# Turning the values product round, with GpSimd normalising, in a two-layer windowed-attention kernel

## What is computed

```
h = shift_token(x)                     # the second half of the columns comes from the row before
q, k, v = split(h @ wqkv)              # 8 heads of 64
q, k = rotary(l2norm(q) * qs, l2norm(k) * ksc)
# windows of 128 rows; each looks at itself and at the window before: 256 keys
attn = softmax(mask(8 * q @ k.T))
o = attn @ v
x = x + o @ wo
h = layernorm(shift_token(x)) @ w1 + b1   # 256 -> 2 x 682
a, g = split(h)
x = x + (a * gelu(g)) @ w2 + b2
```

## Time and profile before

| | |
|---|---|
| median of 3 runs | 3229.55 us (3192.76 to 3246.99) |
| profiled execution: span, which is its own time | 3224.0 us |
| TensorE busy | 96% |
| VectorE busy | 76% |
| ScalarE busy | 58% |
| GpSimd busy | 37% |
| mean granted TensorE clock | 0.969 |
| a steady pair of steps (odd and even) | 42.83 us |

### The profile page before, as it was taken

One profiled execution on the slowest core, in us unless ns is written; L12 is line 12 of the kernel. 1 busy time (PEld: TensorE's weight loads), 2 busy tenths in 40 slices (PEclk: granted clock), 3 DMA queues, 4 the chain that ended last, 5 costly groups with the idle time before them and its releaser, 6 DMA issues.

```text
span 3224.0 us, 71318 instructions
## 1 busy us (share of the span) xinstructions
PE 3082.3 (96%) x23040; PEld 2745.2 (85%) x23040; DVE 2444.6 (76%) x7393; ACT 1877.0 (58%) x4750; POOL 1190.4 (37%) x1303
## 2 busy tenths in 40 slices
PE   8999799999999999999999999999999999999997
PEld 6777588988888898989888888988898888889896
DVE  3566687777777777878777788878787878788885
ACT  3455365665565665656655666656566656566663
POOL 3455343333333333323233334334343344343342
PEclk7799899999999999999999999999999999999998
DMA  4344400000000000000002211001010011010000
GB/s 139 111 138 156 157 25 20 23 24 21 23 24 21 22 20 23 24 21 23 22 23 77 80 42 31 28 26 31 24 30 28 27 31 31 24 31 27 27 28 17
DMA packets 139639, 137.09 MB, mean 43 GB/s; under 512 B 15256, under 2 KB 124912, under 8 KB 137968
## 3 DMA queue, kind: packets, MB, share of 16 engines
q1 hardware_dynamic: 139248, 132.18, 13.0%
HBM read 80.22 MB, written 51.92 MB: 41 GB/s over the span
## 4 chain that ended last, share of the span: by engine, by line
PE 66%; DVE 13%; issue 6%; ACT 2%; DVEq 1%; DMA 1%; POOL 1%; SPq 0%; ACTq 0%; POOLq 0%
PE p_values L1320 11%; PE p_wide L95 10%; PE p_wide L97 9%; PE p_wide L96 9%; PE p_turn L1303 5%; PE p_mixed L95 4%; PE p_mixed L96 3%; PE p_mixed L97 3%; PE p_turn L1277 3%; PE p_score L95 2%; DVE prob L1112 2%; DVE rope_sin L1130 2%; DVE rope_cos L1126 2%; PE p_values L1346 1%; PE p_score L96 1%
## 5 line engine op out<-in xcount | busy, mean ns | idle before, releaser
L984 ACT ACTIVATE prob<-prob,least 128x256 f32<-128x256 f32 (+1 forms) x1024 | 495.8, 489 | 373.3 <-DVE least L1112 373.3
L1112 DVE CUSTOM_DVE_ANT_0 prob<-p_score,mask,inv_norm 128x256 f32<-128x256 f32 (+1 forms) x1024 | 417.0, 464 | 145.7 <-issue 145.6
L1320 PEld LDWEIGHTS p_values<-v,pT 128*128 128x128 f32 x3840 | 456.6, 192 | 50.2 <-issue 32.4
L939 POOL TENSOR_TENSOR inv_norm<-norm_clipped,minus_half 128x8 f32<-128x8 f32 x256 | 445.5, 1740 | 108.1 <-DVE norm_clipped L1141 87.3
L1320 PE MATMUL p_values<-v,pT 128*128 128x64 f32 x3840 | 463.2, 273 | 21.8 <-DVE o L1152 19.7
L95 PE MATMUL p_wide<-hT_h,w_h 128*128 128x256 f32 (+1 forms) x1408 | 408.7, 290 | 15.1 <-DVE gated L1225 12.6
L97 PE MATMUL p_wide<-hT_h,w_l 128*128 128x256 f32 (+1 forms) x1408 | 396.3, 281 | 0.0
L96 PE MATMUL p_wide<-hT_l,w_h 128*128 128x256 f32 (+1 forms) x1408 | 395.8, 281 | 0.0
L999 ACT ACTIVATE pT<-p_turn 128x512 f32<-128x512 f32 (+1 forms) x512 | 266.0, 568 | 174.6 <-PE p_turn L1303 174.6
L1225 DVE SCALAR_TENSOR_TENSOR gated<-p_wide,columns,gelu 128x256 f32<-128x256 f32 (+1 forms) x384 | 184.2, 482 | 231.2 <-ACT gelu L1031 231.2
L95 PE MATMUL p_wide<-wqkv_h,xT_h 128*128 128x512 f32 x768 | 351.4, 458 | 5.0 <-DMA wqkv_l<-w_low 3.8
(11 more groups left out here) (139 smaller groups left out, 8077.8 us busy)
## 6 DMA issues: line engine op xcount, KB each, us to landing
x_tile<-x_rows SPq DMA_DIRECT2D x192, 128.0 KB, 2.1
w_high<-a_wraw_h SPq DMA_DIRECT2D x32, 264.0 KB, 2.2
w_low<-a_wraw_l SPq DMA_DIRECT2D x32, 264.0 KB, 2.5
x_rows<-a_x SPq DMA_DIRECT2D x64, 128.0 KB, 1.7
x_tile<-x_rows SPq DMA_DIRECT2D x128, 64.0 KB, 1.9
mid_rows<-x_mid SPq DMA_DIRECT2D x128, 64.0 KB, 1.6
x_mid_shifted<-mid_rows SPq DMA_DIRECT2D x128, 64.0 KB, 1.9
x_rows<-x_new SPq DMA_DIRECT2D x64, 128.0 KB, 1.7
```

The lines of the kernel that those rows point to most:

```text
L939: pool.tensor_tensor(r[:, slot, heads], rt[:, heads], half[:, heads], ALU.pow)\
L984: act.activation(prob[:, h, cols], prob[:, h, cols], ACT.Exp, bias=least[:, h:h + 1], scale=-1.0, accum_out=rsum[:, h:h + 1]).then_inc(act ...
L1112: dve.tensor_tensor_reduce(prob[:, h, cols], p_score[h % 2][:, c0 + cols.start:c0 + cols.stop], mask[:, a.slot(2), cols], r[:, a.slot(2), ...
L1320: ins = pe.matmul(p_val[:, hh * D:(hh + 1) * D], pT[:, group, hh, b], v[:, slot, h * D:(h + 1) * D], start=b == blocks[0], stop=b == block ...
```

## The change

- Values product: v is the stationary operand (128 keys x 64 columns) and the turned probabilities the moving one (128 columns). Even heads write partitions 0 to 63, odd heads 64 to 127, so o comes out turned, two heads to a block of 128 columns; the turning of o and its multiplication on VectorE go.
- GpSimd multiplies the probabilities by the reciprocals in place (`normalised`), four heads at a time; `prob` has two buffers, and the turning of the probabilities, their copies and the values product move from tile a to tile c, one step later. GpSimd also does the clip of the squared norms.
- Scores: the products of two heads alternate.
- FFN tail: the high and low parts of the 42-row chunk of w_2 are stacked in one 128-row operand, with the high part of the gated activations written twice by ScalarE; two products of 128 rows in place of three of 42. The weights' tail arrives by two transfers more.
- The order of the step changes on all four compute engines. TensorE: probabilities 0 to 3 turned; k's projection in one piece; q and k turned; second FFN product; values 0 to 3; scores 0 to 3; probabilities 4 to 7 turned; q's projection; values 4 to 7; scores 4 to 7; half of v's projection; output projection; the other half; h or x turned; in even steps the first FFN product.

```diff
@@ gpsimd
+                def inverse_norms(n):
+                    heads = slice(n * H, (n + 1) * H)
+                    pool.wait_ge(dve_ss[n], t.done(1, 1))
+                    pool.sem_inc(pool_took, 1)
+                    pool.tensor_scalar(rt[:, heads], ss[:, heads], NORM_FLOOR, None, ALU.max).then_inc(pool_rt[n], 1)
+                    pool.wait_ge(pool_rt[n], t.done(1, 1))
+                    pool.tensor_tensor(r[:, t.slot(2), heads], rt[:, heads], half[:, heads], ALU.pow)\
+                        .then_inc(pool_r[n], 1)
+                def normalised(group):
+                    cols = key_columns(a)
+                    pool.wait_ge(dve_rinv, a.done(2, group + 1))
+                    pool.sem_inc(pool_took, 1)
+                    for h in range(4 * group, 4 * group + 4):
+                        p = prob[:, a.slot(2), h, cols]
+                        pool.tensor_scalar(p, p, rinv[:, h:h + 1], None, ALU.mult).then_inc(pool_p, 1)
...
@@ gpsimd, order of a step: k's rotary sum, inverse norms and scaling (t); layer norm (g);
   last norm (e, layer 1); normalised(0); inverse_norms(0); residual (c); normalised(1)
@@ scalar, order of a step
+                if c:
+                    turned_probs(0)
+                if t:
+                    squares(1, pe_k)
                 if a:
                     ... qT_h, kT_h
+                if c:
+                    turned_probs(1)
                 if a:
                     probabilities(0, 4)
+                if t:
+                    squares(0, pe_q)
+                if c:
+                    act.wait_ge(pe_pv, c.done(2, 2))
+                    act.activation(oT_h[:], p_val[:].rearrange("p (k t) -> p k t", t=P), ACT.Copy).then_inc(act_oT, 1)
                 if a:
+                    probabilities(4, 8)
...
                     def high(n):
...
+                        if n == HF:
+                            act.wait_ge(pool_zero, 1)
+                            act.activation(gT_h[GR:GR + HR, n], gt[0:HR, n % 3], ACT.Copy)
@@ vector, order of a step: rotary(1); qT_l, kT_l; squared_norms(1); x_new; statistics; least_of(0);
   h_norm; last output; rotary(0); oT_l; sums_inverted(0); least_of(1); squared_norms(0); q_rot; x_mid;
   sums_inverted(1); even: hT, hT_l, gated and low parts; odd: xT_l
+                def sums_inverted(group):
+                    heads = slice(4 * group, 4 * group + 4)
+                    dve.wait_ge(act_exp, a.done(H, 4 * group + 4))
+                    need(dve, pool_p, a.done(H, 4 * group - 4))
+                    dve.reciprocal(rinv[:, heads], rsum[:, heads]).then_inc(dve_rinv, 1)
@@ tensor, scores
-                    for h in range(4 * group, 4 * group + 4):
-                        rows, m, c0 = slice(h % 2 * D, (h % 2 + 1) * D), h // 2, h % 4 // 2 * 2 * P
-                        kh, kl = (x_[rows, m].rearrange("p b t -> p (b t)")[:, cols] for x_ in (kT_h, kT_l))
-                        ins = three_pass(pe, p_score[h % 2][:, c0 + cols.start:c0 + cols.stop],
-                                         (qT_h[rows, m], qT_l[rows, m]), (kh, kl), True, True)
+                    for m in (2 * group, 2 * group + 1):
+                        c0 = m % 2 * 2 * P
+                        for q, k, first, last in ((qT_h, kT_h, True, False), (qT_h, kT_l, False, False),
+                                                  (qT_l, kT_h, False, True)):
+                            for half in range(2):
+                                rows = slice(half * D, (half + 1) * D)
+                                ins = pe.matmul(p_score[half][:, c0 + cols.start:c0 + cols.stop], q[rows, m],
+                                                k[rows, m].rearrange("p b t -> p (b t)")[:, cols],
+                                                start=first, stop=last)
@@ tensor, values
-                            ins = pe.matmul(p_val[:, hh * D:(hh + 1) * D], pT[:, group, hh, b],
-                                            v[:, slot, h * D:(h + 1) * D], start=b == blocks[0], stop=b == blocks[-1])
+                            for half in range(2):
+                                h = 4 * group + 2 * m + half
+                                ins = pe.matmul(p_val[half * D:(half + 1) * D, (2 * group + m) * P:(2 * group + m + 1) * P],
+                                                v[:, slot, h * D:(h + 1) * D], pT[:, group, 2 * m + half, b],
+                                                start=b == blocks[0], stop=b == blocks[-1])
@@ tensor, second FFN product
+                    for n in range(HF):
+                        three_pass(pe, p_mix[:, 0:E], (gT_h[:, n, c0:c0 + P], gT_l[:, n, c0:c0 + P]),
+                                   (w2[0][:, n], w2[1][:, n]), n == 0, False)
+                    pe.matmul(p_mix[:, 0:E], gT_h[:, HF, c0:c0 + P], w2[0][:, HF], start=False, stop=False)
+                    pe.matmul(p_mix[:, 0:E], gT_l[:, HF, c0:c0 + P], w2[0][:, HF], start=False, stop=True)\
+                        .then_inc(pe_w2, 1)
```

More of the change, by code:

```diff
@@ L902, in step @@
             def step(st_):
[L903 to L910, removed]
@@ L1064, in step, with least_of @@
                     turned_x(t)
+                def least_of(group):
+                    cols = key_columns(a)
+                    dve.wait_ge(pe_s, a.done(2, group + 1))
+                    if group == 0:
+                        dve.wait_ge(pool_r[0], a.done(1, 1))
+                    at = 2 * a.slot(2) + group
+                    dve.memset(took[:, at:at + 1], 0.0)
+                    for h in range(4 * group, 4 * group + 4):
+                        c0 = h % 4 // 2 * 2 * P
+                        dve.tensor_tensor_reduce(prob[:, a.slot(2), h, cols],
+                                                 p_score[h % 2][:, c0 + cols.start:c0 + cols.stop],
+                                                 mask[:, a.slot(2), cols], r[:, a.slot(2), h:h + 1], BIG,
+                                                 ALU.add, ALU.min, least[:, h:h + 1]).then_inc(dve_least, 1)
@@ new lines, in rotary @@
+                def rotary(n, raised, last):
+                    dve.wait_ge(act_sq[n], t.done(1, 1))
+                    need(dve, last, t.done(1))
+                    if n == 1 and t.is_number(LAYER):
+                        dve.wait_ge(tab_in, 16)
+                    bank = p_wide[1 - n]
+                    src = bank[:].rearrange("p (h s d) -> p h s d", h=H, s=2)
+                    table = tab[:, t.window].rearrange("p c (s d) -> p c s d", s=2)
+                    dve.tensor_tensor(rope_a[:, n], bank[:].rearrange("p (h d) -> p h d", h=H),
+                                      tab[:, t.window, 2 * n].unsqueeze(1).to_broadcast([P, H, D]), ALU.mult)
+                    dst = rope_b[:, n].rearrange("p h (s d) -> p h s d", s=2)
+                    for s in range(2):
+                        ins = dve.tensor_tensor(dst[:, :, s], src[:, :, 1 - s],
+                                                table[:, 2 * n + 1, s].unsqueeze(1).to_broadcast([P, H, D // 2]),
+                                                ALU.mult)
+                    ins.then_inc(raised, 1)
@@ L1065, in step @@
+                if t:
+                    rotary(1, dve_kr, pool_k)
                 if a:
```

319 lines of the change are left out of this document (130 added, 189 removed).

## The result

The changed kernel takes **3719.64 us** (median of 4 runs, 3711.12 to 3739.45) against 3226.69 us for the kernel before on the same chip (3192.76 to 3246.99): ratio 1.1587, 95% interval 1.1518 to 1.1657, slower. Forecast were 3650 us in a range of 3430 to 3820. The profiled execution has a span of 3709.5 us and a mean granted clock of 0.906 (before 3224.0 us and 0.969).

What follows compares the result with a forecast made beforehand. TensorE's own work, busy 96% of the span, was taken as the bound. Over 64 pairs of steps: 3224 + 64 x (10.0 exposed waits - 5.0 saved + 1.7 clock) = 3650 us, range 3430 to 3820.

Steps and rivals of the forecast that it cites:

- Theory 2: The experiments' alternative explanation: the new parts themselves set the pace, GpSimd's multiplication above all; no chance given.
- the three chains: Chains to oT_l, x_mid and hT_l, which the new order leaves uncovered on TensorE: 2.5+1.2, 2.4 and 3.2 us a pair.
- start of a step (gated, xT_l): At a step's start one turning covers too little of the gelu-and-gate or x chain: 0.4 + 0.3 us a pair.
- work saved: TensorE time saved per pair: values 2.7 us, turning o 0.8, FFN tail 0.8, K in one piece 0.4.
- clock: TensorE's clock falls to half behind the wait for hT_l, slowing the FFN products: +1.7 us a pair.
- Wait 1: Output projection waits for oT_l behind ScalarE's and VectorE's queues: 2.5 us in odd steps, 1.2 in even ones.
- Wait 2: TensorE's turning of h or x waits for x_mid behind VectorE's least operations: 1.2 us, twice a pair.
- Wait 3: First FFN product waits for hT_l with nothing in between, 0.4 us of it from GpSimd interference: 3.2 us a pair.
- The clock that stays up: Rival: TensorE's clock does not fall behind the waits, giving 3544 us; chance 0.16.
- Column halves in turn: Rival: the values product's column halves run one after the other, 0.85 us more a group, 3760 us; chance 0.13.
- GpSimd's chain in layer 1: Rival: at 0.73 us a head GpSimd's multiplications delay layer 1's norms for VectorE, giving 3735 us; chance 0.15.
- The faster case: Rival: TensorE stays the bound, waits under 5.0 us a pair, likeliest 3100 us; chance 0.08.

Runs made afterwards that it cites:

- e3: Changed kernel with GpSimd multiplying only 8 columns of each head's probabilities instead of 256: 3680.78 us, ratio 1.1433.
- r5: Changed kernel, all parts kept, queues reordered in several rounds, the last putting xT_l two places earlier in odd steps: 3268.45 us, ratio 1.0109.
- e6: Kernel before with only the turning of h and its follow-up work moved to right ahead of the first FFN product: 3460.02 us, ratio 1.076.
- r2: r1 with the x load behind the store of x_mid, and the last reciprocal deviation and last output later: 3325.31 us, ratio 1.0328.
- e5: Kernel before with the turned values product alone, o neither normalised nor turned, order unchanged: 3168.12 us, ratio 0.9855.
- e7: Changed kernel with 14 filler products in the wait for hT_l and GpSimd multiplying only 8 columns per head: 3539.94 us, ratio 1.1005.
- r1: Changed kernel with all parts kept and only the order of the four engines' queues and their waits changed: 3516.48 us, ratio 1.0918.

## Why the prediction was right, step by step

**The mechanism was right.** The new order cost more than the new parts saved. Theory 2 fell with e3 (the multiplications shortened, 50 us gained of 513) and r5 (same parts, 3268 us); e6 shows one of the three chains causing half of the loss in a kernel that has none of the new parts.

| term, us per pair | forecast | measured | from |
|---|---|---|---|
| wait for oT_l (odd + even) | 2.5 + 1.2 | 4.0; 2.46 and 1.28 in the pair shown | 255.8 / 64 |
| wait for x_mid | 2.4 | 0.95 | (43.0 + 17.7) / 64 |
| wait for hT_l | 3.2 | 2.9 | 184.5 / 64 |
| start of a step (gated, xT_l) | 0.7 | 0.6 | (23.4 + 16.1) / 64 |
| TensorE idle, all | +9.7 (10.0, less 0.3 of old waits) | +8.1 | (623.4 - 107.8) / 64 |
| work saved | -4.7 | -4.0 | r2's pair at the full clock, 38.8 against 42.8 |
| clock | +1.7 | +3.5 to +4.0 | 42.25 - 38.8 in the pair shown; over all pairs, what of the 4.0 saved does not show in TensorE's busy time |
| sum | +6.7 | +8.0 | (3368.3 - 2854.9) / 64 |

- *Wait 1* came out within 0.1 us in the pair shown, in both kinds of step, from queues read instruction by instruction, and 0.3 too small over all pairs; the table load directly behind the copies of pT shows above.
- *Wait 2* is 1.03 us in the even step shown, 1.2 forecast (its own terms, 3.5 less 2.1, give 1.4). In odd steps it mostly does not show: the clock had fallen, TensorE needed 2.5 us for the output projection and not 1.4, and x_mid was there when v's second half ended; 17 waits at the turning of x are left. The prediction had counted wait 2 in full and the odd step's clock at nothing because the one takes the other's place. It does: the two terms together were forecast at 2.4 + 1.7 = 4.1 us and measured at 4.4 to 4.9. That the row of x_mid is too large and a good part of the clock's row too small is one thing under two names.
- *Wait 3* has its second part where it was put, but on another neighbour: hT_l took 1.24 us beside GpSimd's residual add and not beside a multiplication.

```profile
1243.55 0.99 DVE L1219 TENSOR_SCALAR hT<-p_mixed,columns 128x256 f32<-128x256 f32 x2 [0.67 <-PE p_mixed L1427]
1245.24 1.24 DVE L1224 TENSOR_TENSOR hT_l<-hT,hT_h 128x512 fp32r<-128x512 f32 x1 [0.69 <-ACT hT_h L1040]
```

```profile
1245.21 0.72 POOL L969 TENSOR_TENSOR residual<-x_mid,b_rows 128x256 f32<-128x256 f32 x1
```

0.69 us is what it takes undisturbed (the shortest of the 64, 0.693), so 0.5 are lost where 0.4 were forecast.
- *The clock was mis-sized*: 3.5 to 4.0 us and not 1.7. It falls behind two waits in a pair, the odd one for oT_l as well (clock 0.55 from 1271.8), whose part I had set to nothing beside wait 2.
- *The saving was overrated*: 4.0 us and not 4.7. The values group (1.02 for 1.06) and the tail (0.39 twice) are as costed, and alternating scores gave nothing, as said. In e5, the values and the turning of o give 2.9 us a pair of busy time for the 3.5, which is most of what is missing. K in one piece was not separated.
- *GpSimd's multiplication* was outside both of my bounds: 0.94 us for 128x256 in the mean (0.905 with the 128 of half the width) and not 0.36 to 0.73. A step's eight and two clips come to 7.6 us, not 4.4. It did not move the sum far because its results are needed a step later: a multiplication of 0.34 us instead gains some 50 us by the second phases of e3 and e7, 0.8 us a pair.

Idle time came out 1.6 us a pair lower than forecast, the saving 0.7 smaller and the clock some 2 dearer. In the second phase the sum was therefore 84 us short (513 against 64 x 6.7 = 429). The time was only 70 us off, 60 by the profiled executions, and that is partly luck: in these the untouched first phase took 28 us less in the changed kernel than in the one before.

**Rivals.** The clock that stays up fell (0.906). Column halves in turn fell (1.02 us a group). GpSimd's chain in layer 1 fell, though its multiplication was longer than that rival needed and its 3735 us is nearer to the measured time than 3650: between pass ends a pair takes 50 to 51 us in layer 0 and 51 to 53.5 in layer 1, so most of the loss is already in layer 0. The faster case would have needed waits under 5.0 us a pair; in this order there were 8.1.

**Open.** Whether any order lets the new parts win was not shown: r5 is still 1.1% above the kernel before (0.1 to 2.1%). e5 says that in the old order VectorE's chains are what stands next. The waits for oT_l and x_mid were not put into the kernel before by themselves, as e6 does with the one for hT_l; for them the evidence is the changed kernel's own trace and that r1 to r5 shorten them.

## What to carry to other kernels

A kernel whose bound engine is busy for 96% has its other queues arranged around that work; before taking work from it, find how far the second chain is behind, since in e5 184 us less work for TensorE made the phase 52 us shorter. When an order is changed, walk each engine's queue from the producer to the consumer: the two waits at oT_l could be forecast within 0.1 us in the pair shown that way, and moving one turning by four groups cost 7.6% by itself. Count a clock loss for every bare wait of 2 to 3 us, and not only for the longest: counted in the changed kernel's second phase, the mean granted clock of the stretch behind the wait, as long as the two shown above, was under 0.9 for all 59 waits of 2.6 to 3.2 us, for 72 of the 94 of 2.0 to 2.6 us, and for 14 of the 90 of 1.0 to 1.5 us. And before a mean clock or a busy time of two executions is compared, take out the part that the change does not touch: here it alone took 341 to 400 us, at clocks of 0.94 to 0.78.

## What the runs showed of the hardware that was not expected

- GpSimd's multiplication of 128x256 float32 by one number per partition, in place, takes 0.94 us in the mean (four in 3.65 where nothing holds them up), longer than its two-input add of the same size (0.73), and of 128x8 still 0.338.
- The clock need not be down when the first product starts behind a wait: behind 3.02 us of idle the products ran 0.12 us apart for 1 us and only then 0.21 apart for 3.4 us; behind 2.46 us they were 0.21 apart from the start.
- VectorE's sum for q_rot, two SBUF inputs, has a median of 904 ns beside GpSimd's full multiplications and 682 ns in e3, beside the short ones; hT_l goes from 0.69 to 1.24 us beside one residual add. By the Trainium skill (SBUF — State Buffer, Who interferes with whom) only the port pair that VectorE shares with GpSimd makes engines wait for each other; these two rows, both VectorE operations with two SBUF inputs beside GpSimd, agree as far as they go, and that nothing else does no run here shows.
- Products of 64 output rows in the two column halves run together just as the row halves of the scores do: 16 in 1.02 us.
